# Two-layer adaLN FFN on one core: the loads and the split of low rank B in the opening, issued and placed differently

## The reference

```python
h = gelu(embedding @ W0 + b0); h = gelu(h @ W1 + b1)
att = softmax(h @ W2 + b2)                       # one row of 8 weights for each batch
agg_w = einsum('bk,koi->boi', att, weight)       # each batch's own 32x32 mixing matrix
y = einsum('boi,bih->boh', agg_w, x) + (att @ bias_k)[:, :, None]

def qlinear(v, q, scale, A, Bm):                 # 4-bit weights, low rank term of rank 32
    return v @ ((q - 7.5) * (scale * 0.005)[:, None]).T + 0.02 * (v @ A @ Bm)
x = x + qlinear(silu(qlinear(y, gate...)) * qlinear(y, up...), down...)
# second layer: grouped convolution of 9 taps + context, then an fp8-rounded 512x512 matmul, added to x
```

## Time and profile before

| | us |
|---|---|
| median of three runs (lowest, highest) | 375.62 (375.14, 377.08) |
| the profiled execution's own time | 375.3 |
| its span, first to last instruction | 373.5 |
| TensorE busy | 362.5 (97% of the span) |
| VectorE busy | 246.9 (66%) |
| ScalarE busy | 190.3 (51%) |
| GpSimd busy | 93.1 (25%) |

### The profile page before, as it was taken

How to read it: one execution, slowest core, us unless ns; L and a number is a source line. 1 busy time by engine, 2 the same in 40 slices (tenths; PEclk the granted TensorE clock), 3 DMA queues, 4 the chain that set the end, 5 groups by cost and what they waited for, 6 DMA issues and landing times.

```text
span 373.5 us, 5792 instructions
## 1 busy us (share of the span) xinstructions
PE 362.5 (97%) x2207; PEld 300.6 (80%) x2208; DVE 246.9 (66%) x399; ACT 190.3 (51%) x345; POOL 93.1 (25%) x78
## 2 busy tenths in 40 slices
PE   7999999999999999999999999999999999998994
PEld 3777887899888879998888889988888899997231
DVE  4959999626576664273766652647889922588995
ACT  4676698303555563135555550335667511066972
POOL 2101433311242224111333241113233221142040
PEclk9999999999999999999999999999999999999998
DMA  6889575296320000222200000426000299977188
GB/s 222 309 181 372 163 252 192 85 326 120 47 44 0 0 0 3 41 45 42 43 0 2 2 0 13 72 43 154 0 3 1 57 283 270 195 182 182 72 193 259
DMA packets 82475, 41.72 MB, mean 112 GB/s; under 512 B 52416, under 2 KB 72784, under 8 KB 82320
## 3 DMA queue, kind: packets, MB, share of 16 engines
q1 hardware_dynamic: 69072, 37.70, 36.9%
q10 hardware_dynamic: 12624, 1.82, 3.1%
q0 software_dynamic: 752, 1.84, 2.5%
HBM read 26.55 MB, written 14.80 MB: 111 GB/s over the span
## 4 chain that ended last, share of the span: by engine, by line
PE 77%; DVE 8%; ACT 6%; DMA 3%; issue 3%; POOL 1%; DVEq 0%; SPq 0%
PE ps L673 33%; PE ps L658 24%; PE ps L688 4%; PE ps L708 3%; PE ps L868 3%; PE ps L606 3%; DMA lr_b<-lr_b_rows 2%; PE ps L710 2%; PE ps L664 1%; ACT mix L937 1%; PE ps L848 1%; DVE a_buf L1423 1%; DVE a_buf L1413 1%; DVE b_buf L1416 1%; PE ps L621 1%
## 5 line engine op out<-in xcount | busy, mean ns | idle before, releaser
L1137 POOL TENSOR_TENSOR h_lo<-a_buf,h_hi 128x512 fp32r<-128x512 f32 (+1 forms) x44 | 57.5, 1308 | 122.2 <-ACT h_hi L979 122.2
L658 PE MATMUL ps<-down_w,h_hi 128*128 128x288 f32 (+1 forms) x352 | 76.3, 298 | 0.6 <-POOL h_lo L1137 0.4
L658 PE MATMUL ps<-down_w,h_lo 128*128 128x288 f32 (+1 forms) x352 | 74.8, 293 | 0.0
L673 PE MATMUL ps<-x_hi,gate_w 128*128 128x512 f32 (+1 forms) x176 | 69.9, 397 | 0.0
L673 PE MATMUL ps<-x_hi,up_w 128*128 128x512 f32 (+1 forms) x176 | 69.6, 396 | 0.0
L673 PE MATMUL ps<-x_lo,gate_w 128*128 128x512 f32 (+1 forms) x176 | 69.6, 395 | 0.0
L673 PE MATMUL ps<-x_lo,up_w 128*128 128x512 f32 (+1 forms) x176 | 69.2, 393 | 0.0
L658 PEld LDWEIGHTS ps<-down_w,h_hi 128*128 128x128 f32 (+1 forms) x352 | 57.2, 189 | 2.1 <-POOL h_lo L1137 0.7
L658 PEld LDWEIGHTS ps<-down_w,h_lo 128*128 128x128 f32 (+1 forms) x352 | 56.1, 188 | 0.0
L1423 DVE TENSOR_TENSOR a_buf<-a_buf,b_buf 128x512 f32<-128x512 f32 (+1 forms) x44 | 50.0, 1136 | 8.9 <-ACT a_buf L1043 7.8
L1147 POOL TENSOR_TENSOR x_nat<-y_buf,x_nat 128x512 f32<-128x512 f32 x15 | 20.7, 1383 | 94.9 <-DVE y_buf L1309 94.9
(11 more groups left out here) (194 smaller groups left out, 488.1 us busy)
## 6 DMA issues: line engine op xcount, KB each, us to landing
x_nat<-in_x SPq DMA_DIRECT2D x4, 1024.0 KB, 6.6
out<-x_nat SPq DMA_DIRECT2D x15, 256.0 KB, 4.2
turned<-x_nat SPq DMA_DIRECT2D x12, 256.0 KB, 3.3
x_nat<-in_down_q SPq DMA_DIRECT2D x11, 256.0 KB, 3.3
x_nat<-in_gate_q SPq DMA_DIRECT2D x10, 256.0 KB, 5.8
x_nat<-in_up_q SPq DMA_DIRECT2D x10, 256.0 KB, 5.9
edges<-zeros SPq DMA_DIRECT2D x4, 512.0 KB, 9.8
xt_own<-turned SPq DMA_DIRECT2D x6, 256.0 KB, 3.4
```

The lines of the kernel that those rows point to most:

```text
L658: last = mm(ps[:, 4 + 2 * (j % 2) + m, 0:HALF + R], part[0:k, ic, j * P:(j + 1) * P], down_w[0:k, ic, m, :], start=first, stop=end)
L673: last = mm(ps[0:k, bank(ic, 2 * m), :], w[:, H * ic + c * k:H * ic + (c + 1) * k], part[:, c, :], start=c == 0 and part is x1_hi, stop=c ...
L1137: nc.gpsimd.tensor_tensor(h_lo[0:k, ic, :], a_buf[0:k, ic % 2, :], plain(h_hi[0:k, ic, :]), ALU.subtract).then_inc(h_lo_ready, 1)
```

## The change

Three loads leave SyncE's list and are issued by ScalarE, behind its first table load: low rank B first, then the first tile of x, then low rank A. ScalarE's copy of low rank B to its high part moves from behind the additive term's copy to just behind the exponential, so ahead of `att_hi`; GpSimd's subtraction waits for that copy as before and moves with it. SyncE's store of the two parts moves ahead of the slots 4 to 7.

```diff
--- before.py
+++ after.py
@@ -457,15 +457,12 @@
             sp.dma_start(cond_w_left[:], cond_w_rest).then_inc(mixw_in, 16)
             sp.dma_start(ident[:], ident_in).then_inc(ident_loaded, 16)
             sp.dma_start(bias_k_sb[:], bias_k).then_inc(bias_k_in, 16)
-            sp.dma_start(x_nat[:, 0:TG, :], x_tile(x, 0)).then_inc(x_in[0], 16)
-            sp.dma_start(stage_lr_a[:].rearrange("p c m r -> p (c m r)"), lr_a).then_inc(lr_in, 16)
 
             def load_slot(n):
                 if n >= RING:
                     sp.wait_ge(q_ready, n - RING + 1)
                 sp.dma_start(slot(n), slot_dram(n)).then_inc(q_in[n % RING], 16)
 
-            sp.dma_start(stage_lr_b[:].rearrange("p m n -> p (m n)"), lr_b).then_inc(lrb_in, 16)
             for n in range(4):
                 load_slot(n)
             sp.dma_start(gate_sc[:], gate_s).then_inc(scale_in, 16)
@@ -473,12 +470,12 @@
             sp.dma_start(stage_ctx_w[:], ctx_w).then_inc(ctx_in, 16)
             sp.dma_start(stage_side[:], fside).then_inc(ctx_in, 16)
             sp.dma_start(stage_mask[:], batch_mask).then_inc(ctx_in, 16)
-            for n in range(4, RING):
-                load_slot(n)
             sp.wait_ge(lrb_hi, 1)
             sp.wait_ge(lrb_ready, 1)
             sp.dma_start(lr_b_rows.rearrange("m v r (c n) -> (r c) m v n", n=LRC),
                          plain(lr_b_parts[:])).then_inc(lrb_stored, 16)
+            for n in range(4, RING):
+                load_slot(n)
             sp.wait_ge(lrb_stored, 16)
             for half in range(2):
                 sp.dma_start(plain(lr_b4[half * 2 * R:(half + 1) * 2 * R]),
@@ -883,6 +880,9 @@
 
             act.wait_ge(const_set, 1)
             load_table(0, ACT.Gelu)
+            act.dma_start(stage_lr_b[:].rearrange("p m n -> p (m n)"), lr_b).then_inc(lrb_in, 16)
+            act.dma_start(x_nat[:, 0:TG, :], x_tile(x, 0)).then_inc(x_in[0], 16)
+            act.dma_start(stage_lr_a[:].rearrange("p c m r -> p (c m r)"), lr_a).then_inc(lr_in, 16)
             act.wait_ge(cond_in, 16)
             act.wait_ge(h0_mm, 1)
             activation(h0[:], ps[:, 0, 0:B], ACT.Gelu, bias=b0_sb).then_inc(h0_act, 1)
@@ -891,6 +891,8 @@
             load_table(1, ACT.Exp)
             act.wait_ge(soft, 2)
             activation(probs[:], logits[:], ACT.Exp, bias=stat[:, 0:1], accum_out=stat[:, 1:2]).then_inc(exp_done, 1)
+            act.wait_ge(lrb_in, 16)
+            activation(lr_b_parts[:, :, 0, :], stage_lr_b[:], copy).then_inc(lrb_hi, 1)
             act.wait_ge(att_tr, 2)
             activation(att_hi[:], ps[0:STACKED, 3, 0:B], copy).then_inc(att_hi_ready, 1)
 
@@ -922,8 +924,6 @@
             activation(lr_a_w[:, :, :, 0, :], stage_lr_a[:], copy).then_inc(lra_hi, 1)
             act.wait_ge(aggb_mm, 1)
             activation(agg_b[:, 0:TILE], ps[:, BIAS_BANK, :], copy).then_inc(aggb_ready, 1)
-            act.wait_ge(lrb_in, 16)
-            activation(lr_b_parts[:, :, 0, :], stage_lr_b[:], copy).then_inc(lrb_hi, 1)
             act.wait_ge(mix_ready, 2)
             activation(mix_kept[:], ps[:, MIX_BANK, :], copy).then_inc(mix_saved, 1)
             split_mixed(0)
```

## The result

The changed kernel takes 382.14 us (median of five runs, 382.09 to 383.18) against 375.62 us before, a ratio of 1.0172 with a 95% interval of 1.0152 to 1.0191. It is slower by 6.5 us; the forecast was 375.0 with a range of 374.0 to 377.0. Its profiled execution took 382.09 us, with a span of 380.3 and a granted clock of 0.984 over all (before: 375.3, 373.5 and 0.997).

A forecast was written before the change was run, and what follows sets the result against it. The prediction took TensorE, busy nearly all the time, as the bound, so only its stalls count. Terms -0.34 - 0.88 + 0.56 = -0.66 us moved the median from 375.62 to 375.0 us, range 374.0 to 377.0.

The forecast's parts named there:

- The three issues on ScalarE: Between 2.24 and Gelu at 4.24, ScalarE's three load issues, at most 1.98 us, fit at no cost.
- The arrival of x: x, issued at about 2.7, arrives at 12.3, just under the 12.51 TensorE reaches anyway: cost 0.
- the case of 12.3: x sharing the DMAs with slots 0 to 3, adding 3.0 us to an arrival of 9.3.
- The clock: Opening: a fall to 1.2 GHz would cost more than all three terms; no chance given.
- -0.34: TensorE's hole at L664 on x_lo closes as GpSimd's subtraction leaves 13.70: -0.34 us.
- -0.88: TensorE's stall at L688 goes because low rank B's load back arrives by 26.1: -0.88 us.
- 1.22: The gain in us from both stalls, at L664 and L688, going.
- +0.56: `condition(0)` (L606) starts at 12.51 instead of 11.95, `att_bias` being held by GpSimd's moved subtraction: +0.56 us.
- a shift at L688 goes through to the end: The 0.66 us gained on TensorE at L688 carries through to the kernel's end.
- C: Rival: x is the last prerequisite, arriving at 13.3; L606 1.35 us late, 375.8 us; chance 0.15.
- D: Rival: ScalarE's issues are held like SyncE's 1.40, Gelu 0.55 us late, 375.5 us; chance 0.07.
- E: Rival: low rank B late (9.1), ScalarE waits ahead of `att_hi`, net +1.0, 376.6 us; chance 0.08.

The follow-up runs named there:

- e5: Changed kernel with ScalarE's three load issues moved one wait lower, behind the wait for `cond_in`, same order; 376.98 us, ratio 1.0043.
- e1: Changed kernel with x and low rank A back on SyncE behind `bias_k`, low rank B still on ScalarE; 378.17 us, ratio 1.0053.
- e7: Changed kernel with only its moved loads; ScalarE's split and the store back in their old places; 382.04 us, ratio 1.0178.
- e11: Changed kernel with SyncE issuing low rank B, x, low rank A behind `bias_k`, and `att_bias` reading PSUM; 375.55 us, ratio 0.9979.
- e2: Changed kernel with ScalarE issuing low rank B, low rank A, then x last; 380.17 us, ratio 1.0116.
- e6: Changed kernel with ScalarE sending x as four transfers of 256 KB in place of one; 380.77 us, ratio 1.0139.
- e9: Changed kernel with ScalarE's issues behind the wait for `cond_in` and `att_bias` reading its factor from PSUM bank 3; 376.99 us, ratio 1.0029.
- e12: Kernel with all loads on SyncE and `att_bias` from PSUM, plus nine instead of six warm-up matmuls behind the logits; 375.39 us, ratio 0.999.
- e10: Changed kernel with ScalarE's issues behind the wait for `cond_in` and GpSimd's subtraction held until `att_bias` is done; 377.48 us, ratio 1.0022.
- e8: Changed kernel with only its split and store; the three loads back on SyncE, low rank B last; 381.27 us, ratio 1.0158.
- e3: Changed kernel with VectorE's two steps on the mixing weights moved behind the attention weights `att`; 380.54 us, ratio 1.0123.

## Why the prediction was wrong

**The step that failed is "The three issues on ScalarE", with "The arrival of x" behind it.** The first took ScalarE as free at 2.24, behind its table load, and costed the issues at nothing because they fit into ScalarE's gap. They start at 1.04, while the table load runs from 0.75 to 2.03, and so the loads come ahead of `cond_w_left` (1.65) and `ident` (2.10). Issued at 2.24 and later, as the prediction had it, they would have come behind both, as in e5 (3.40 to 4.29), where `cond_w_left` takes 3.0 us; no run issued them at 2.24. The second step asked only when x and low rank A arrive and what SyncE's slots take from them. It never asked what x takes from loads that SyncE had already in hand, and so had no row for `cond_w_left`, although VectorE's first work waits for it with the logits queued behind, and TensorE's wait for VectorE's attention weights (`att`) stood in the view of the earlier trace rows with 0.5 us. The price of a transfer on a second queue includes what it takes from the loads of the first one. That was +4.4 us at the logits where the sum had 0, shown by e5 (same queue, later issue: gone), e1 (x on the other queue, later issue: most of it gone) and e7 (the loads alone: the whole loss).

The rule quoted there, "DMA: Bandwidth & Descriptors", section "Queues, rings and completion order" of the Trainium skill, has each DMA engine take turns between the queues. The trace agrees from 2 to 3 (45.4% for SyncE's queue, 42.5% for ScalarE's) and doesn't from 4 to 7: in 5 to 6 it is 100.8% for ScalarE's queue against 2.1% for SyncE's, when both had transfers issued. By an estimate from even turns the 128 KB of `cond_w_left` would have waited for about as much of x, 0.4 us at 346 GB/s. How large a packet in that rule's sense is here, no run shows, so the rule itself may stand with very uneven turns. The rule was used for x only, as the case of 12.3, and not for what x displaces.

**The clock** stood in the last paragraph as a way to spoil the sum, with no chance of its own. It came true inside the wait of 4.7 us and cost 3.14 us by the account; in e11 the runs with a lower clock are 1.7 or 3.0 us slower. That the wait brought it on is likely and not shown. All four runs of e7, which has the wait, and four of the five of the changed kernel have a granted clock of 0.984 to 0.986, and the kernel before is at 0.991 or above in all of its 69 runs beside the experiments. But e2 and e6, with waits of 1.7 and 1.2 us, have runs at 0.985 and 0.986 as well, the clock falls in e5, e9, e11 and e12 without any wait over 0.9 us, and in 52 of those 69 runs of the kernel before it reads 0.991 to 0.995. The fifth run of the changed kernel reads 0.996 and is the slowest, 383.18 us; whether it stayed at half rate through the opening, like e10, is not known, since it has no trace.

**-0.34 and -0.88 were right in size, but the changed kernel doesn't show it.** Neither stall is in it, and the stretch from the first L670 to L685 is 1.31 us shorter, where 1.22 was forecast. But TensorE came there 6 us late, and e7, with the split and the store in their old places, has the same stretch in 11.72 us. Being late was enough to hide both stalls, so for the changed kernel the agreement is luck in part: its store was issued at 14.21, not at 10.0. The terms are borne out by e5 and e11. In e11 the first L673 is only 1.42 us later than before, the store is issued at 10.16, the load back lands at about 25.3, where L688 is at 28.67, and the stretch takes 11.71 us.

**+0.56 was right as a mechanism and wasn't paid.** `att_bias` took 1.23 us in place of 0.68 and ended at 14.66, 0.54 us behind GpSimd's end at 14.12, as in the earlier trace rows. But L588 ran at 1.2 GHz until about 15.3, and L592 started at 15.27 without a wait. In e5, where the clock was still up, it was paid: `att_bias` again ends 0.54 us behind GpSimd, and TensorE waits 0.59 us ahead of L592 for it. In e11, where `att_bias` isn't held, the four fastest runs are 1.0 to 1.4 us below the fastest of the kernel before, where the two stalls alone would give 1.22.

**That a shift at L688 goes through to the end was right:** +6.10 there, +6.07 at 111.56, +6.06 at the chain's last matmuls, and 6.5 in the medians.

**Of the rivals** none was it. C had x late, D had ScalarE late, E had low rank B late; none had a load of SyncE's late. E's price was 1.0 us net, for low rank B at 9.1. e8, which has its condition, is 5.9 us slower than before: low rank B comes at 10.4, which by E's own sum makes it about 2.3, and the clock falls there too.

What stays open is what makes the clock fall at about 12 us in e5, e9, e11 and e12, and what sets the moment at which the half rate of the start ends. The idle time ahead of L592 is not it (e9 has none). The idle time ahead of L584 is not enough: e12 has 0.27 us there and the kernel before has 0.48. The same kernel on the same chip takes 373.9 us with a granted clock of 1.0 in one run and 375.6 with 0.991 in another (e11).

## What to carry to other kernels

When a large load is moved to an engine that can issue it earlier, list every load that is issued after it and waited for before it lands, on all queues, and find who stands behind those waits; the price is theirs. In an opening where TensorE lives between short waits, cost each new wait twice, once for itself and once for the row of matmuls that may run at the lower clock behind it, here 1.7 to 3 us. The moment of issue is worth a line in the sum of its own: one semaphore wait ahead of the three issues was worth 4.9 us, and taking them off ScalarE, where they stood ahead of the first Gelu, another 1.4. And when a stall is gone after a change, look whether it is gone too in a run that has only the delay: here it was.

## What the runs showed of the hardware

- ScalarE issues DMAs while its table load runs: 1.04, 1.48 and 1.96 us inside a load of 0.75 to 2.03.
- Two hardware queues do not share evenly in the opening. A load of 128 KB issued 0.17 us behind one of 1,024 KB on the other queue took 7.3 us in place of 2.9; issued 0.31 us ahead of it, with 128 KB more ahead on the other queue, 4.9 (e2). It isn't a strict order either: `cond_w_left` landed at 8.96, x at 11.3. And the engines weren't full: from 4 to 5 the two queues together had 66.5% of their time, and SyncE's only 2.9%. Which rule of service gives this was not found.
- GpSimd's subtraction holds not only VectorE's products of two SBUF operands (1.50 us, e5; 0.68 with one operand in PSUM, e9): the cast `cond_w_hi`, with a single SBUF input, took 1.84 us in place of 0.68 beside it (e3) and ended 0.54 us behind it.
- The granted clock of the records can miss a stretch at half rate. In all fourteen traces it says 1.00 from the first matmul on, while four clock-keeping matmuls take 1.89 us in place of 1.04; in e10 and e6 it says so beyond 16 us, and eight matmuls take 1.91 us in place of 1.08 there. In e9 the two runs with a clock of 0.999 are the slow ones (378.75 and 378.84 us). Durations of one form of matmul are the safer sign.
